# SyncE's order inside a body: the maxima row ahead of the query reload, the expert weight loads last

## What is computed

```python
x = x + tanh(g_xattn[0]) * xattn(layernorm(x), ctx_1024, ctx_1024, Wq, bq, Wk, bk, Wv, bv, Wo, bo)
x = x + tanh(g_ffn[0]) * moe(layernorm(x), Wr, br, W1, b1, W2, b2)
# moe: logits = xt @ Wr + br; the two best experts of each token, softmax over those two;
#      h = relu(x @ W1[e] + b1[e]); y = h @ W2[e] + b2[e]; sum of the two, weighted
```

## Time and profile before

| | us |
|---|---|
| median of 3 runs | 1007.96 |
| lowest, highest | 1001.5, 1013.3 |
| the profiled execution | 1007.24 |
| its span on the core | 1005.5 |
| TensorE busy | 836.6 (83%) |
| mean granted TensorE clock | 0.887 |

### The profile page before, as it was taken

The page is one execution under the profiler, slowest core; times in us unless marked ns, Lnnn a source line. Parts: engine busy times, 40 slices in busy tenths (PEclk is TensorE's granted clock), DMA queues, the critical chain, the costliest instruction groups (busy, mean ns, idle before and its releaser), DMA issues.

```text
span 1005.5 us, 21803 instructions
## 1 busy us (share of the span) xinstructions
PE 836.6 (83%) x6483; PEld 566.4 (56%) x6484; DVE 549.4 (55%) x980; ACT 419.8 (42%) x777; POOL 514.0 (51%) x463
## 2 busy tenths in 40 slices
PE   4588998999998998873056999999999999999920
PEld 2245555555555555532025777777777777777710
DVE  2356665565655655511495555555555655655557
ACT  2156765666765666551003333333333333333300
POOL 4114766776766766159403355555555555555210
PEclk9699998898998989975557999999999999999975
DMA  3234444444444443314601111111111111111159
GB/s 108 79 87 129 147 144 148 145 147 146 146 144 147 144 146 90 105 43 137 230 0 43 43 48 52 48 47 51 49 42 52 51 43 50 49 47 48 37 192 330
DMA packets 107248, 98.88 MB, mean 98 GB/s; under 512 B 12550, under 2 KB 100044, under 8 KB 107084
## 3 DMA queue, kind: packets, MB, share of 16 engines
q1 hardware_dynamic: 95212, 73.76, 23.7%
q0 software_dynamic: 7488, 20.46, 6.6%
q10 hardware_dynamic: 4512, 4.20, 1.2%
HBM read 67.03 MB, written 31.20 MB: 98 GB/s over the span
## 4 chain that ended last, share of the span: by engine, by line
PE 48%; SPq 24%; DMA 11%; issue 6%; DVE 5%; POOL 4%; ACT 1%; DVEq 0%; POOLq 0%; ACTq 0%
PE banks L1385 19%; SPq L404 14%; DMA k_parts<-kparts 7%; PE banks L1371 7%; PE banks L1373 7%; PE banks L1372 7%; SPq L412 3%; PE banks L1157 2%; PE banks L1358 2%; PE banks L1231 1%; POOL wst L566 1%; DVE hot_col L1037 1%; SPq L478 1%; DMA y2b<-y_rows 1%; POOL wall L568 1%
## 5 line engine op out<-in xcount | busy, mean ns | idle before, releaser
L1385 PE MATMUL banks<-wall,hh 128*128 x624 | 222.7, 379 | 0.5 <-DVE yb L1089 0.5
L818 ACT ACTIVATE hid<-banks,b_col 128x256 f32<-128x256 f32 x312 | 131.0, 471 | 208.1 <-PE banks L1373 112.6
L917 DVE TENSOR_REDUCE negmax<-banks 128x4 f32<-128x1024 f32 x128 | 155.7, 1216 | 81.8 <-PE banks L1198 81.6
L631 POOL DMA_INDIRECT y_rows<-yb,dest_idx x78 | 106.9, 1370 | 160.9 <-DVE yb L1089 137.8
L1371 PE MATMUL banks<-xh,wall 128*128 128x256 f16 x624 | 170.5, 273 | 0.0
L1372 PE MATMUL banks<-xl,wall 128*128 128x256 f16 x624 | 170.5, 273 | 0.0
L1373 PE MATMUL banks<-xh,wall 128*128 128x256 f16 x624 | 170.5, 273 | 0.0
L744 ACT ACTIVATE probs<-banks 128x1024 f32<-128x1024 f32 x128 | 131.1, 1025 | 85.2 <-PE banks L1219 84.0
L1385 PE MATMUL banks<-wall,hl 128*128 x624 | 157.3, 273 | 0.0
L1087 DVE SCALAR_TENSOR_TENSOR yb<-banks,b_b 128x256 f32<-128x256 f32 x78 | 33.1, 424 | 133.0 <-PE banks L1385 133.0
L621 POOL DMA_INDIRECT xg<-xn_rows,gather_idx x78 | 77.3, 991 | 48.2 <-POOL gather_idx L617 32.7
(11 more groups left out here) (159 smaller groups left out, 1289.5 us busy)
## 6 DMA issues: line engine op xcount, KB each, us to landing
wst<-in_L_ffn_W SPq DMA_DIRECT2D x32, 512.0 KB, 4.7
ks<-k_parts SPq DMA_DIRECT2D x192, 32.0 KB, 1.8
qs<-q_parts SPq DMA_DIRECT2D x192, 32.0 KB, 1.8
xin<-in_x SPq DMA_DIRECT2D x16, 256.0 KB, 2.9
cin<-in_ctx SPq DMA_DIRECT2D x16, 256.0 KB, 3.1
k_parts<-kparts SPq DMA_DIRECT2D x16, 256.0 KB, 5.7
q_parts<-qparts SPq DMA_DIRECT2D x16, 256.0 KB, 4.0
xres<-in_x SPq DMA_DIRECT2D x16, 256.0 KB, 2.8
```

The costliest lines, as they stand in the source:

```text
L631: nc.gpsimd.indirect_dma_start(y_d, bass.IndirectOffsetOnAxis(dest_idx[par][:, s:s + 1], 0), yb[par][:, s, :], None).then_inc(y_sent[par], 16)
L818: ins = nc.scalar.activation(hid[half][:, c % (HC // 2), :], banks[:, b, c % 2 * TS:(c % 2 + 1) * TS], ACT.Relu, bias=b1_col[:, ds(e * HC ...
L917: nc.vector.tensor_reduce(negmax[:, c, 8 * (g // 2):8 * (g // 2) + 8].rearrange("p (m g p2) -> p m g p2", m=2, g=2)[:, :, g % 2, :], banks ...
L1385: ins = nc.tensor.matmul(dst, h_[:, c, s * P:(s + 1) * P], w_, start=(c == 0 and k == 0), stop=(c == HC - 1 and k == 1))
```

## The change

Only the order of SyncE's instructions in a body changes; no transfer, no size and no wait is added or removed. The first maxima row is issued between the reload of the keys and the reload of the queries. The result stores follow the query reload as before. The two weight loads, which stood ahead of the key store, now stand behind the result stores.

```diff
                 if last >= 0:
                     late_load(2 + 2 * last)
                     late_load(3 + 2 * last)
+                if ahead:
+                    store_part(m + 1, 1 - par, "k")
+                    store_part(m + 1, 1 - par, "q")
+                    load_part(m + 1, 1 - par, "k", 0)
+                if maxima:
+                    max_row(m, par, 0)
+                if ahead:
+                    load_part(m + 1, 1 - par, "q", 0)
+                if post:
+                    results(m - 2)
                 if weights:
                     for w in range(2):
                         e = t - 1
...
                         sp.dma_start(stage_view(wst[w], w), src).then_inc(w_full[w], 16)
-                if ahead:
-                    store_part(m + 1, 1 - par, "k")
-                    store_part(m + 1, 1 - par, "q")
-                    load_part(m + 1, 1 - par, "k", 0)
-                    load_part(m + 1, 1 - par, "q", 0)
-                if maxima:
-                    max_row(m, par, 0)
-                if post:
-                    results(m - 2)
                 if isinstance(m, int) and m == NB - 1:
```

## The result

The changed kernel takes 1116.03 us in the median (1106.97 to 1123.12, 4 runs) against 1004.73 us before on the same occasions (4 runs): 1.109 of the time before, 95% interval 1.097 to 1.122. It is 11% slower. The forecast was 1110 us, with a range of 1078 to 1145. The profiled execution took 1121.33 us, its span 1119.6.

What follows compares the result with a forecast made beforehand. TensorE, nearly full, and its wait for SyncE were taken to bound the kernel. Four terms, 11.9 + 9.3 + 4.3 + 8.4 = 33.9 us a body, make twelve bodies 102.8 us longer: 1110 us, range 1078 to 1145.

Steps and rivals of the forecast that it cites:

- `high(0)` to the next start: From the weight load's landing to the next body's start: 7.0 us at full clock, 8.9 at half clock, taken as 8.4.
- What bounds the kernel: Bodies 2 to 13, 25.33 us each: TensorE alone needs 22.15, the rest is waiting for SyncE and clock loss after it.
- The swap costs nothing: Maxima row and query reload are both wanted at the next body's start, so the later decides; swap costed at nothing.
- The stall: ScalarE waits at v = 5 for its body's weight load, some 10 us in 12 bodies; TensorE idles 9 us.
- Second term: From `q_split` to SyncE's issue of the first weight load: 9.3 us, including an 8.60 us row of issues.
- Third term: The first weight load until it lands: 4.3 us, the middle between 3.4 in body 9 and 5.3 in body 10.
- First term: Start of a body to `q_split`: 11.9 us, near the full-clock 11.5 of body 3; body 8 took 14.3.
- rival with 0.08: Stall plus clock loss reaching into the next body: 37.8 us a body, +150, 1157 us; chance 0.08.
- What is hidden: Next body's second halves of inputs, issued about 4 us in, wanted about 11 us in: cover 5 us or more.
- From body 14 on: The profile was to show nothing different from body 14 on.

## Why the prediction was right

The mechanism was the one forecast, and the chain closes on the measured body. Means over the twelve bodies, in us:

| term | predicted | measured |
|---|---|---|
| start to `q_split` | 11.9 | 12.9 |
| `q_split` to the issue of the load | 9.3 | 9.4 |
| issue to `high(0)` | 4.3 | 3.8 |
| `high(0)` to the next start | 8.4 | 8.2 |
| body | 33.9 | 34.3 |

- **What bounds the kernel.** Right: with the weight loads placed between the stores SyncE's wait shrinks and a body falls to 22.6 us, against the 22.15 read from body 3.
- **The swap costs nothing.** Right, ratio 0.9998, and for the reason given. That it could be of use once the query reload has to wait for its store was not seen.
- **The stall.** Right in place and size: 12 waits of 9.7 us in the mean where some 10 were forecast, TensorE idle for 8.3 to 9.0. Moving ScalarE's wait takes most of it away, with the transfers left in the changed order.
- **Second term.** Right within 0.1 us, because it was read off as an unbroken series of the trace of before.
- **Third term.** Half a us too long: the load came in near the faster of the two landings of before (3.4 us), although two result stores were issued just ahead of it.
- **First term.** A us too short, and this is the one step whose reasoning was off. I held that the slow clock would lie mostly ahead of the body's start, and took nearly the value of body 3. But body 3 is an exception in the trace of before: there `q_split` came 11.5 and 11.65 us in in bodies 3 and 9 and 13.2 to 14.3 in the ten others, 13.3 in the mean. In the changed kernel, in six of the eleven bodies that follow a stall it reached over it, and `q_split` came 13.5 to 14.3 us in; in the other five 11.5 to 11.6 (body 2, with no stall ahead, 12.9). What I had as a rival with 0.08, the clock loss in the next body, was thus true of about every second body in its first term. The clock's part, 37 us by the run with 16 added matmuls, was in the sum with (8.4 - 7.0) + (11.9 - 11.5) = 1.8 us a body, 22 us. Errors of both signs, not insight, brought the sum within 6 us of the median.
- **What is hidden.** Right: SyncE reached the key store ahead of `k_split` or nearly so, GpSimd waited for ScalarE and not the reverse, and no wait for the second halves appears in TensorE.
- **From body 14 on.** Wrong: nothing different was expected there, and it is 4.6 us, in bodies 14 and 15. The matmuls of the earlier trace rows stand at the end of body 15, not in 16.

## What to carry to other kernels

Before a load is moved back in its queue, find the instruction that uses it and write both as times from the loop's start: here 22 us for the issue (12.9 + 9.4) against 15 for the use, and that alone decides. The gain aimed at (a store without a megabyte ahead of it) was real and could be had one place further on, where the queue waits anyway. And price a stall of TensorE with what the clock costs behind it, 37 us here; but compare with the clock that the kernel had before, not with full clock.

## What the runs showed of the hardware

The clock's return has two sizes. Windows of 1 us in the changed kernel, columns as in the earlier trace rows. The matmuls came back at 244.48 us in body 6 and at 276.92 in body 7, after stalls of 8.66 and 8.81 us:

```profile
246.00:247.00 1.00, 1.00 (x14) 0.29 (x8) 0.00 (x0) 0.50 (x2) 0.77 (x1) 0.50 0.00 0
...
249.00:250.00 1.00, 0.88 (x12) 0.66 (x6) 0.00 (x0) 1.00 (x3) 0.19 (x1) 1.00 0.23 67
...
278.00:279.00 1.00, 0.99 (x9) 0.20 (x8) 0.00 (x0) 0.94 (x2) 1.00 (x1) 0.50 0.00 0
...
288.00:289.00 1.00, 1.00 (x6) 0.31 (x9) 0.00 (x0) 0.04 (x1) 0.91 (x1) 0.50 0.31 38
...
290.00:291.00 1.00, 1.00 (x13) 0.81 (x8) 1.00 (x3) 0.91 (x1) 0.54 (x1) 1.00 0.00 0
```

After the first it was back at 2.4 GHz within 5 us, after the second it stayed at 1.2 GHz for some 12 us, with TensorE busy throughout and the same instructions in the same order. Bodies with the long return took about 3.5 us more between the landing of their load and the next `q_split`. The clock had fallen about 2.4 us into the first of these stalls and about 4.3 us into the second (1 us windows at 0.63 and 0.70). Long and short often alternate: in the run with the weight loads alone `q_split` came 13.98 to 14.22 us into bodies 5, 7, 9, 11 and 13 and 11.58 to 11.59 into the even ones between, but in the changed kernel bodies 8, 9 and 10 all began slowly. What decides between the two stays open; the version with the loads ahead of the result stores, whose stalls are 1.4 us shorter, had the short one in nearly every body.
